# A decoder layer on one core: the order of small steps in the third phase, the bank of the projected values, and the bias in the tail

## The reference, cut to what matters

```
q = x @ WQ; k = enc @ WK; v = enc @ WV
scores = q k^T / sqrt(8); masked or future keys get -1e9
x = layernorm(x + softmax(scores) v @ WO)
```

```
scores = softmax(x @ W_gate); w = top2(scores); w = w / sum(w)
out = x @ W_shared.T + (w0 + w1) * (x @ W_expert.T) + bias
x = layernorm(x + out)
```

## Time and profile before

| what | value |
|---|---|
| median of 3 runs | 563.21 us (560.77 to 564.78) |
| the profiled execution | 561.41 us, span 559.7 us, 22010 instructions |
| busy: TensorE matmul, VectorE, ScalarE, GpSimd | 491.0 (88%), 404.7 (72%), 363.9 (65%), 374.7 (67%) us |
| mean granted TensorE clock | 0.973 of full speed |
| 447.64 to 464.89: busy TensorE, VectorE, ScalarE, GpSimd | 15.97, 14.38, 12.51, 14.30 of 17.25 us |
| granted clock 535 to 550, 550 to 560 | 0.65, 0.50 |

### The profile page before, as it was taken

The page is one execution under the profiler, slowest core; times in us unless marked ns, Lnnn a source line. Parts: engine busy times, 40 slices in busy tenths (PEclk is TensorE's granted clock), DMA queues, the critical chain, the costliest instruction groups (busy, mean ns, idle before and its releaser), DMA issues. The chain is left out here.

```text
span 559.7 us, 22010 instructions
## 1 busy us (share of the span) xinstructions
PE 491.0 (88%) x8800; PEld 365.4 (65%) x8800; DVE 404.7 (72%) x1406; ACT 363.9 (65%) x685; POOL 374.7 (67%) x686
## 2 busy tenths in 40 slices
PE   2899999998999999997899999899998999998750
PEld 1777777775777767774567667676676666766530
DVE  2677777755777776556678878688887888888764
ACT  1566666555777777747777677677677676777432
POOL 6566666645577774833337878778787887879553
PEclk9999999999999999999999999899999999999775
DMA  6530000000000000002000111111201121010001
GB/s 167 169 117 2 3 2 1 4 2 1 2 0 3 1 1 1 2 7 49 17 23 4 50 51 26 28 50 50 49 6 49 51 50 50 5 51 21 22 2 57
DMA packets 24742, 17.38 MB, mean 31 GB/s; under 512 B 2112, under 2 KB 22464, under 8 KB 24640
## 3 DMA queue, kind: packets, MB, share of 16 engines
q1 hardware_dynamic: 24208, 15.90, 10.7%
q10 hardware_dynamic: 432, 0.07, 0.1%
HBM read 11.77 MB, written 4.19 MB: 29 GB/s over the span
## 5 line engine op out<-in xcount | busy, mean ns | idle before, releaser
L783 ACT ACTIVATE gel<-gel,row_scale 128x512 f32<-128x512 f32 x96 | 66.1, 720 | 29.2 <-DVE gel L1056 19.0
L790 ACT ACTIVATE gel<-pair 128x1024 f32<-128x1024 f32 x64 | 51.8, 809 | 29.0 <-PE pair L1414 28.5
L1354 PEld LDWEIGHTS pair<-w,gel 128*128 128x128 f32 x512 | 60.4, 192 | 8.0 <-issue 5.7
L1043 DVE TENSOR_REDUCE neg_max<-pair 128x16 f32<-128x1024 f32 x64 | 60.5, 945 | 5.1 <-PE pair L1368 5.0
L1354 PE MATMUL pair<-w,gel 128*128 128x128 f32 x512 | 62.4, 276 | 1.0 <-ACT gel L715 1.0
L1318 PE MATMUL pair<-hT,w 128*128 128x512 f32 x128 | 58.3, 596 | 1.3 <-ACT lev L710 1.3
L1414 PE MATMUL pair<-ident,gel 128*128 128x128 f32 x384 | 55.7, 280 | 2.9 <-ACT gel L783 1.9
L532 POOL TENSOR_SCALAR k_exp<-k_sb,quad_mask 128x512 f32<-128x512 f32 x64 | 43.0, 690 | 20.8 <-ACT k_sb L762 12.7
L1414 PEld LDWEIGHTS pair<-ident,gel 128*128 128x128 f32 x384 | 43.4, 141 | 19.1 <-issue 13.5
L1368 PE MATMUL pair<-k_exp,qT 32*32 32x128 f32 (+1 forms) x2048 | 44.5, 333 | 2.6 <-issue 2.4
L509 POOL TENSOR_TENSOR X<-X,proj_sb 128x512 f32<-128x512 f32 x16 | 20.3, 1270 | 35.6 <-ACT proj_sb L673 35.6
(11 more groups left out here) (138 smaller groups left out, 1221.9 us busy)
## 6 DMA issues: line engine op xcount, KB each, us to landing
X<-in_x SPq DMA_DIRECT2D x16, 256.0 KB, 3.1
cT<-in_ctx SPq DMA_DIRECT2D x16, 256.0 KB, 3.9
out_rows<-X SPq DMA_DIRECT2D x15, 256.0 KB, 2.4
mask_rows<-in_mask_early SPq DMA_DIRECT2D x16, 128.0 KB, 3.6
w<-in_L_attn_w SPq DMA_DIRECT2D x2, 256.0 KB, 3.4
out_rows<-X SPq DMA_DIRECT2D x2, 128.0 KB, 1.8
w_kv<-in_L_attn_wk SPq DMA_DIRECT2D x1, 64.0 KB, 3.3
w_q<-in_L_attn_wq ACTq DMA_DIRECT2D x1, 64.0 KB, 3.1
```

Of the source, the lines that this page charges most:

```text
L783: nc.scalar.activation(part, part, ACT.Exp, scale=row_scale[:, n:n + 1])\
L790: nc.scalar.activation(pT[par].rearrange("p (a c) -> p a c", a=2), turned, ACT.Copy)\
L1043: nc.vector.tensor_reduce(neg_max[par][:, :].rearrange("p (a h) -> p a h", a=2), scores, AX.X, ALU.max, negate=True).then_inc(max_ready, 1)
L1354: last = nc.tensor.matmul(bank(6 + q)[:, P * t:P * (t + 1)], gel[:, q, f, P * t:P * (t + 1)], w_2[:, f, :], start=(f == 0), stop=(f == NF ...
```

## The change

- **Values.** `project_v` makes 16 matmuls of 64 columns in place of 4 of 128: for each of the 8 batches of a group, the two halves of the heads go to the two halves of the partitions. The result goes to bank 5, where k was (it waits for `k_ready`), and `copy_v` becomes two activations of 64 x 512.
- **y.** `turn_y` and `copy_y` move from tile 0 of slot s (for group s + 1) to tile 3 (for group s + 2). On TensorE it stands in front of y2's turn, on ScalarE behind y2T's copy.
- **Mixture in phase 3.** `MOE_BANK` changes; in tile 3 only the copy of product 0 is left, the copies of products 1 and 2 move to tile 0 of the next slot behind `copy_pT`, and product 3 moves from behind `turn_probabilities` to behind `scores_open`, its copy behind attT's. The second product of tile 3 now waits for yT. `gate_top` moves behind the `xattend` of tile 0.
- **Tail.** The products of groups 14 and 15 (`moe_biased`) add the bias by a second matmul, identity times bias. GpSimd's mixture of 14 and bias of 15 go; VectorE mixes 14; the rows of 13 go from ScalarE to GpSimd (`last_norm`); VectorE's statistics of 14 move ahead of the weights of 15.

```diff
-MOE_BANK = [5, 6, 4, 5]
+MOE_BANK = [6, 4, 5, 5]
...
             def end():   (GpSimd)
-                mixture(LAST - 1, q)
-                end_offset(LAST - 2, rstd_c, offs_b[0])
+                last_norm(LAST - 2, LAST % 2)
                 end_offset(LAST - 1, rstd_b[1], offs_b[1])
-                add_bias(LAST, 2)
                 pool.wait_ge(ln_c.done, LAST - 1)
                 ln_deviation(pool, ln_c, LAST, mv_c, veps_c, rstd_c)
 
             def end_offset(g, rstd, offs):
                 ln_deviation(pool, ln_c, g, mv_c, veps_c, rstd)
+                pool.wait_ge(ln_c.done, g)
...
             def copy_v(g, q):   (ScalarE)
                 after(act, pv_done, g * TG - TG)
                 act.wait_ge(xv_done, g + 1)
-                values = bank(first_bank(g, 4)).rearrange("p (u h i e) -> p u h i e", u=TG, h=2, e=DH)
-                for b in range(2):
-                    for h in range(2):
-                        batches = v2[q][h * S:(h + 1) * S, :, :, h, 0:DH] \
-                            .rearrange("p (u b) i e -> p u b i e", b=2)
-                        last = nc.scalar.activation(batches[:, :, b, :, :],
-                                                    values[b * S:(b + 1) * S, :, h, :, :], ACT.Copy)
+                for h in range(2):
+                    rows = slice(h * S, (h + 1) * S)
+                    last = nc.scalar.activation(
+                        v2[q][rows, :, :, h, 0:DH],
+                        bank(first_bank(g, 5))[rows, :].rearrange("p (b i e) -> p b i e", i=HH, e=DH),
+                        ACT.Copy)
                 last.then_inc(v2_ready, 1)
...
                     if exists(s):   (ScalarE, phase3)
                         copy_pT(s * TG + t, t % 2)
+                    if s == 0 and t == 0:
+                        copy_y(1)
                     if t == 0 and exists(s - 2):
-                        collect((s - 2) * TG + TG - 1, TG - 1, p)
+                        for u in range(1, TG - 1):
+                            collect((s - 2) * TG + u, u, p)
                     if t == 0 and exists(prev):
                         act.wait_ge(xatt_xposed, prev + 1)
                         after(act, xproj_done, prev)
                         nc.scalar.activation(attT[:, :], bank(6), ACT.Copy).then_inc(xattT_ready, 1)
-                    if t == 0 and exists(nxt):
-                        copy_y(nxt)
+                    if t == 0 and exists(s - 2):
+                        collect((s - 2) * TG + TG - 1, TG - 1, p)
                     if t == TG - 1 and exists(prev):
                         act.wait_ge(y2_xposed, prev + 1)
                         after(act, moe_done, prev * TG)
                         nc.scalar.activation(y2T[:, :], bank(6), ACT.Copy).then_inc(y2T_ready, 1)
+                    if t == TG - 1 and exists(s + 2):
+                        copy_y(s + 2)
...
                     if t == TG - 1 and exists(prev) and s < LAST:
-                        for u in range(TG - 1):
-                            collect(prev * TG + u, u, q)
+                        collect(prev * TG, 0, q)
...
-                    if t == 0 and exists(old):   (VectorE, phase3)
-                        gate_top(old, p)
                     if t == 0 and exists(s + 1):
                         future_keys(s + 1, q)
                     if t == 0 and exists(s):
                         after(dve, xatt_xposed, s - 1)
                         xattend(n, p, t)
+                    if t == 0 and exists(old):
+                        gate_top(old, p)
...
                 gate_weights(LAST - 1)   (VectorE, end)
+                mixture(LAST - 1, q)
                 gate_top(LAST, 2)
+                last_statistics(LAST - 1, q)
                 gate_weights(LAST)
-                last_statistics(LAST - 1, q)
                 mixture(LAST, 2)
...
             def project_v(g, q):   (TensorE)
-                for u in range(TG):
-                    last = nc.tensor.matmul(bank(first_bank(g, 4))[:, P * u:P * (u + 1)],
-                                            cT[q][:, P * u:P * (u + 1)], w_xv[:, :], start=True, stop=True)
+                for u in range(2 * TG):
+                    for h in range(2):
+                        last = nc.tensor.matmul(bank(first_bank(g, 5))[h * S:(h + 1) * S,
+                                                                       FH * u:FH * (u + 1)],
+                                                cT[q][:, S * u:S * (u + 1)],
+                                                w_xv[:, FH * h:FH * (h + 1)],
+                                                start=True, stop=True)
...
+            def moe_biased(g, t):
+                nc.tensor.matmul(bank(t)[:, 0:2 * D + NE], y2T[:, P * t:P * (t + 1)], w_moe[:, :],
+                                 start=True, stop=False)
+                nc.tensor.matmul(bank(t)[:, 0:D], ident[:, :], bias_bc[:, :], start=False, stop=True)\
                     .then_inc(moe_done, 1)
...
                     if exists(s):   (TensorE, phase3)
                         turn_probabilities(n, t)
-                    if t == 0 and exists(s - 2):
-                        pe.wait_ge(moe_ready, (s - 2) * TG + 1)
-                        moe(s - 2, TG - 1)
+                    if n == 0:
+                        turn_y(1)
                     if t == 0 and exists(r):
                         pe.wait_ge(xatt_ready, r * TG + TG)
-                        after(pe, moe_ready, (s - 1) * TG - 2)
+                        after(pe, moe_ready, (s - 1) * TG - 3)
                         turn_attended(q, 6, range(TG))
-                    if t == 0 and exists(g):
-                        after(pe, moe_ready, (s - 1) * TG - 1)
-                        after(pe, v2_ready, g)
-                        turn_y(g)
...
                     if t == 2 and exists(g):
+                        pe.wait_ge(k_ready, g + 1)
+                        project_v(g, q)
+                    if t == 3 and exists(s + 2):
                         pe.wait_ge(q_ready, g + 1)
-                        project_v(g, q)
+                        turn_y(s + 2)
...
                         scores_open(n + 2, n + 3)
+                    if t == 0 and exists(s - 2):
+                        pe.wait_ge(moe_ready, (s - 2) * TG + 3)
+                        moe(s - 2, TG - 1)
                     if exists(s):
...
                         for u in range(TG - 1):
+                            if u == 1 and exists(g):
+                                pe.wait_ge(yT_ready, min(s + 3, NG))
                             if u == 2 and exists(g):
                                 pe.wait_ge(v2_ready, g + 1)
                             moe(r, u)
```

More of the change, by code:

```diff
@@ L841, in phase3 @@
                     if t == TG - 1 and exists(prev) and s < LAST:
-                        for u in range(TG - 1):
-                            collect(prev * TG + u, u, q)
+                        collect(prev * TG, 0, q)
             def end_rows(g, q, rstd, offs):
-                act.wait_ge(end_offs, g - LAST + 3)
+                act.wait_ge(end_offs, 1)
                 for t in range(TG):
@@ L853, in end @@
             def end():
-                p, q = LAST % 2, 1 - LAST % 2
+                q = 1 - LAST % 2
                 (k0, first), (k1, second) = halves
-                for u in range(2):
-                    collect((LAST - 1) * TG + u, u, q, u)
+                collect((LAST - 1) * TG, 0, q, 0)
                 act.wait_ge(xatt_xposed, NG + 1)
                 copy_half(4, attT, second)
-                for u in range(2, TG):
+                for u in range(1, TG):
                     collect((LAST - 1) * TG + u, u, q, u)
@@ L872, in end @@
                 gate_exp(LAST)
-                end_rows(LAST - 2, p, rstd_c, offs_b[0])
                 end_rows(LAST - 1, q, rstd_b[1], offs_b[1])
@@ L1095, in mixture @@
             def mixture(g, p):
-                dve.wait_ge(bias_ready, g + 1)
+                if g == LAST - 2:
+                    dve.wait_ge(bias_ready, g + 1)
                 for t in range(TG):
@@ L1134, in phase3 @@
                         shift(1, 1)
-                    if t == 0 and exists(old):
-                        gate_top(old, p)
                     if t == 0 and exists(s + 1):
@@ L1457, in project_v, with moe @@
             def project_v(g, q):
-                for u in range(TG):
-                    last = nc.tensor.matmul(bank(first_bank(g, 4))[:, P * u:P * (u + 1)],
-                                            cT[q][:, P * u:P * (u + 1)], w_xv[:, :], start=True, stop=True)
+                for u in range(2 * TG):
[5 more added lines that the diff above has]
+                                                start=True, stop=True)
                 last.then_inc(xv_done, 1)
-            def moe(g, t, dst=None):
-                nc.tensor.matmul(bank(MOE_BANK[t] if dst is None else dst)[:, 0:2 * D + NE],
+            def moe(g, t):
```

(26 more changed lines are left out.)

## The result

The changed kernel takes 567.59 us (median of 6 runs, 566.43 to 569.69) against 562.12 us (6 runs) for the one before: ratio 1.010, 95% interval 1.0065 to 1.0135. It is 1% slower, 5.5 us between the medians; 5.4 was forecast. The profiled execution has a span of 564.7 us against 559.7.

What follows compares the result with a forecast made beforehand. A 17.25 us slot cycle through VectorE, ScalarE and GpSimd was the bound, one through TensorE close below. Profiled 561.4 + 8.4 (slots) - 3.0 (tail) = 566.8; median 563.2 + 5.4 = 568.6 us, range 558 to 575.

Steps and rivals of the forecast that it cites:

- path A: Third-phase slot's cycle through TensorE: 16.61 us before, 0.64 to spare in the slot shown, 17.86 after the change.
- The steady slot: One third-phase slot: 17.86 us from 17.25, 0.6 longer, with bounds of +0.4 and +0.9.
- O: End of VectorE's subtraction for the fourth tile of a slot, from which later steps are timed.
- The slots' sum: Third phase: 13 slots of 0.6 (7.8), pauses 0.5, less 0.2, last slot's first tile 0.35: +8.4 us.
- Values: Slot's value step: two copies shorten path B by 0.1; 16 products cost 0 (0 to +0.3 a slot).
- y's turn: Moved from first to fourth tile: products there wait, +0.21 us on path A; first tile's opening gains about 0.1.
- path B: Slot's cycle from O through ScalarE's exp and value copies, GpSimd's spread and mixture, to VectorE's statistics: holds 17.25 us.
- Fourth product, gate: First tile, path A: product between opening and values +0.35 us; gate's top behind the attention adds 0.69 of VectorE.
- The tail: After the slots: VectorE's mixture of 15 comes 3.0 us earlier, last products grow 0.9: -3.0 (-1.5 to -3.5).
- Rivals 1 and 2: Path B keeps holding the slot: 558.9 us (chance 0.22); with the copies' full 0.4 counted, 555.0 us (0.07).
- rival 3: Value products become TensorE's bound in the slot, each slot 0.5 longer at 2.4 us: 575.1 us, chance 0.09.
- rival 4: Tail gives nothing, its last products growing by more than 1.0 us: 571.6 us, chance 0.05.

Runs made afterwards that it cites:

- t3: Changed kernel with product 3 (in bank 4), the copies of products 1 and 2 and the gate's top back in their old places: 556.76 us.
- u3: Kernel before with values' and tail's edits, GpSimd adding the bias of group s - 1 in its idle time before ln_c's deviation: 552.55 us, ratio 0.9867.
- u2: Kernel before with the values' edits (bank left as it was) and the tail's edits, without early y or the mixture's moves: 556.13 us.
- v3: u3 with the early turn of y and the values in k's bank: 554.50 us, ratio 0.9874 to the kernel before.
- u1: Changed kernel with product 3 (in bank 4) and copies of products 1 and 2 back, gate's top left behind the first tile's attention: 561.78 us.
- t4: Changed kernel with the gate's top alone put back in front of the attention of a slot's first tile: 567.30 us.
- t1: Kernel before with the tail's edits alone: 557.54 us, ratio 0.9908 to the kernel before.
- u4: Kernel before with one more matmul of 128 columns, its result unread, behind each of the tail's eight products: 563.17 us, ratio 1.0014.
- v1: Kernel before with GpSimd's mixture of group 14 held in the tail until VectorE has written y2's second half: 560.47 us, ratio 0.9987.
- t2: Kernel before with the values' edits alone, 16 products and two copies, bank left as it was: 559.80 us, ratio 0.9962.
- v2: u3 run once more, beside v3: 555.79 us, ratio 0.9882 to the kernel before.

## Why the prediction was right

**What holds the slot.** Right. Two cycles, 17.25 by GpSimd and 16.6 to 16.85 by TensorE, were read from one slot; t3, u2 and u3 show both, one after the other, as the slot's length. My 16.61 for path A left out that the row maximum also waits for the closing of the scores; with it, it is 16.85. The waits came as forecast too: 0.78 in front of the reciprocal (0.5 to 0.8), and still one in front of the statistics.

**The steady slot, 17.86 forecast, 18.03 measured.** Term by term: O (466.36 here) to the next turn 6.08 (6.05 forecast), turn to opening 2.15 (2.2), opening to product 0.91, product 0.64 (0.44), values to reciprocal 0.87 (0.97), reciprocal to gate 0.50, gate to row maximum 0.77 (0.69), row maximum to O 6.11 (6.11). The term that was sized wrong is the product: it costs 0.20 more between scores and values than between a turn and a turn. The weight loads wait 0.35 before it and 0.34 behind it, where before there was one such wait between opening and values. That agrees with the Trainium skill (TensorEngine Tiling (Array Packing), Key Properties: a change of tiling mode drains the array), since the product is a 128 x 128 tile between two of other shapes; what no run separates is how much of each wait is the drain.

**The slots' sum, +8.4.** The profiles have +10.6 to the turn of slot 15, 1.0 of it before slot 2, where a pause of 0.51 in TensorE's matmuls (286.91) falls in. Thirteen times the difference of the undisturbed slots, 18.02 - 17.24 = 0.78, is 10.1. Pauses differ between two executions by some microseconds, so this sum isn't tested to better than that.

**Values.** Right: two copies take 1.26, the path lost 0.1 to 0.2 by it, and the products were covered.

**y's turn.** Right in its terms: y2T's copy waits 0.28, the second product's loads wait 0.19 for yT. On path A it takes 0.24 there (6.08 against 5.84) and gives back 0.14 at the opening (2.15 against 2.29): 0.1 a slot, which is what v3 shows. Where path B holds the slot (t3) no cost shows.

**Fourth product, gate.** Right as the cause, shown by u1, t4 and t3. I hadn't said that the two are tied: with the product late the gate's place is worth nothing in time (t4), with the product early it is worth 0.4 to 0.5 a slot (u1 to t3).

**The tail, -3.0: mis-sized, it measured -5.1 (t1), -5.6 between the spans.** The removed steps were right, but two terms had the wrong size. First, I let the last two products grow by 0.9 for their bias. From the start of y2T's last copy to the end of the last product's copy before took 543.65 - 540.66 = 2.99, after takes 2.46. Windows of before and of after around those products, the granted clock third from the end:

```profile
540.00:544.00 4.00, 2.75 (x6) 1.40 (x6) 2.21 (x18) 1.16 (x3) 1.39 (x2) 0.50 0.00 0
```

```profile
551.00:555.00 4.00, 1.10 (x7) 0.82 (x6) 3.52 (x20) 1.01 (x3) 3.41 (x7) 1.00 0.00 0
```

Before, TensorE had stood idle for 2.10 us ahead of the last turns (idle before 539.94, for VectorE's xn rows) and ran at the lower of its two clock levels (1.2 GHz); after, the last turns (549.60) follow without a gap, and it ran at the upper one (2.4 GHz). By u4, of this 1.4 us against the forecast about 1.0 is the clock and 0.4 that the added matmuls cost less than 0.9. u4 (idle for 1.45) and v1 (1.31) lost the clock as before did; that the closed gap is what kept it is argued from these, not tested by a run that changes the gap alone. Second, I took VectorE's own steps as they stood, and two of them held pauses beside GpSimd's operations: 0.86 in the xn rows, 0.6 in the copy inside the gate's top (from its start to the statistics' 0.80 after, 1.45 to its end in the forecast). Both go when GpSimd's mixture goes; v1 shows it for the first of them, and shows the second come back longer where the addition still runs beside it. And what was late next was not the last product, as I had it: its copy ends at 552.53, and the gate's top starts at 553.14, when VectorE's own mixture of 14 (552.08, 1.1) is through. VectorE's queue is the bound there now. Part by part, from the second attended turn of the tail (533.85 before, 544.38 after) to the end of VectorE's last rows (557.42 and 562.46):

| up to | before | after | gain | forecast |
|---|---|---|---|---|
| start of y2T's last copy | 6.81 | 5.69 | 1.12 | 0 |
| end of the last product's copy | 2.99 | 2.46 | 0.53 | -0.9 |
| gate's top of 15 | 0.10 | 0.61 | -0.51 | 0 |
| VectorE's mixture of 15 | 8.07 | 3.42 | 4.65 | 3.9 |
| end of VectorE's last rows | 5.60 | 5.90 | -0.30 | 0 |
| sum | 23.57 | 18.08 | 5.49 | 3.0 |

Against the forecast the products gave 1.4 and the pauses 1.5 (0.86 in the first part, 0.6 in the fourth), and smaller steps 0.4; VectorE's queue took back 0.5, and 0.3 went at the end, where GpSimd's deviation of 15 now waits for ScalarE's rows of 14 (559.96).

So the mechanism was right, but that the total came right to 0.1 us is luck: a slot loss sized some 2 us too small met a tail gain sized some 2 us too small. Rivals 1 and 2 (path B goes on holding) are out by the slot, rival 3 (the value products) by t2, rival 4 by t1.

## What to carry to other kernels

An idle gap in front of a step may be the slack of one cycle or room in another: work that fills a gap at one engine is free only if the next step there isn't the one for which another engine waits. Add up both cycles before moving a step, and price it at its new place, with the tile shapes beside it. And look which operations of another engine lie beside a step that takes longer than its like elsewhere: removing those gave the tail 1.5 us on top of the removed steps.

## What was not expected of the hardware

While GpSimd ran its operation with two SBUF inputs (538.28, 1.26 us), the first of VectorE's two xn rows, begun at 538.42, took 1.21 us, and the second started at 539.55, 0.01 after GpSimd's end; alone, such a row takes 0.34. The line of the two rows (ns, shortest/median/longest), and the chain of waits of before:

```profile
L357 DVE TENSOR_SCALAR xn<-X,mv_b,rstd_b x2: 336/771/1206, 538.4 to 539.5; 128x128 f32<-128x128 f32 x2
```

```profile
538.42 0.12 DVE xn L357
538.54 1.01 issue
539.55 0.35 DVE xn L357
```

The Trainium skill (SBUF — State Buffer, SBUF: two separate sides) states it: VectorE and GpSimd share a pair of ports, and of a GpSimd operation and a VectorE one that needs the pair (in a 2-port mode, or with two SBUF inputs) whichever starts first holds it for its whole instruction. This case's traces agree for GpSimd's operations with two SBUF inputs: in before, t2 and u4 (1.46 us for the two rows each) and, with the operation moved away, in v1 (0.60), and in the gate's copy (0.78 before, 1.02 in v1, 0.81 to 0.95 in the slots of v2; 0.17 otherwise). They do not show it for GpSimd's rows L340: in after the same copy starts nine times while such a row (0.44) runs, and takes 0.17 in six of them and 0.19 to 0.33 in three. The profile counts the standing still as busy time of the grouped row and as "issue" in the chain, so it is easily taken for the instruction's own length.
